# One operand of a seven-product matrix scheme gets a buffer of its own, two others are made at later tiles

## The chip, the cores and the metric

The kernel runs on one core of a Trainium2 chip. The metric is the device time of one execution in microseconds (us), here the median of several runs. "The trace" is one execution recorded by the hardware profiler; its times count from the first instruction.

## What is computed

For each of 8 batches of 512 tokens with 2048 features, a linear layer with a per-batch low-rank adapter is followed by a gated feed-forward block, and the input is added at the end:

```python
h   = x @ W.T + bias + (x @ A.T) @ B.T          # W: 2048x2048, A, B: rank 16, chosen by batch
q   = h @ Wq.T                                  # router: top 8 of 512 slots, softmax, values
aux = softmax(top8(...)) @ values @ Wvd.T @ Wvu.T
u   = 0.5 * log1p(var(h)) / mean(log1p(var)) + 2.5 * sigmoid(gelu(h @ Wu1.T + bu1) @ Wu2.T + bu2)
out = x + h + gate(u) * aux
```

All of it is in fp32. Only the first line matters for the change.

## The kernel before, in words

**The scheme.** W is cut into 2 x 2 blocks of 1024 x 1024. Two batches form a pair, so that x is a 2 x 2 block matrix too, and h is made with seven block products instead of eight, from sums and differences of blocks. There are four pairs. Each pair runs the products in the order M1, M2, M6, M7, M4, M5, M3 (lines 45 and 46), and each product has 8 output tiles of 128 rows. A tile g (0 to 223, `tile_of(g)` gives pair, product, tile) is 8 steps of k with three matmuls each (lines 1781 to 1783), since each fp32 operand is split into a high and a low part: high x high, high x low, low x high. The first tile of M1, M2, M7 and M4 also carries two matmuls of the adapter for each k (lines 1721 and 1722), and the tile after each tile of M2, M4, M5 and M3 carries one (line 1709).

**Differences of weight blocks.** M6, M7, M4 and M5 need differences of W's blocks, called T2, T3, T4 and T1. They are made once, in the first pair, in 8 pieces of 128 x 1024 (512 KB) each, and three of the four go to DRAM (`t_dram`) for the later pairs. `t_res` (32 KB a partition) holds W's first block for M1; `make_t1(o)` (line 1265) turns its piece o into T1, which ScalarE's queue stores (`store_t1`, line 895); `make_t2(o)` (line 1270) turns it into T2, which stays for M6. `make_t4(o)` (line 1275) computes T4 from a block of W and T2; `store_t4` (line 899) stores it; it is read again for M4. `make_t3(o)` (line 1280) makes T3 in the place of the tile's own weights, and `split_w_hi` stores it.

**The ring of raw weights.** All pieces of W, the loads for T1, T2 and T4 among them, go through `wraw`, a ring of three places of 512 KB. The list `entries` (lines 363 to 373) sets their order by due tile; load n goes to place n mod 3 and waits in SyncE's queue (`load_w`, line 531) until what lay there is used: for T1 and T2 until VectorE has made them, for T4 and T3 until their store to DRAM has landed (`wait_stored`, line 389). SyncE issues all loads in one order: at step g the `wraw` loads that are due by g + 1, a piece of `t_res` while g is under 6, the loads of x up to a given entry, and the adapter's. What waits first holds all behind it.

**A step of the engines.** Every engine runs its own list, tile by tile; its part for tile g is called step g here. ScalarE at step g writes the high part of the weights of tile g + 2 (`split_w_hi`, line 877; it waits until tile g - 1 is done, since `wsp` has three places), stores and squares the output of tile g - 2, stores T1 and T4 of step g - 1, and writes high parts of x for the next product (`PREP_AT`: k = 0, 1, 2, 3 at tiles 1, 2, 3, 5 of a product, k = 4 to 7 at its last tile). VectorE at step g adds up the outcome of tile g - 1 (`combine`), writes the low part of the weights of tile g + 2 (`split_w_lo`), makes the T pieces that are due, writes the low parts of x (`split_x_lo`), adds the sums of tile g - 2 to `sums` (`add_sums`, line 1349) and finishes tile g - 1 (`finish`, line 1328) where it is a tile of h. GpSimd makes the sums and differences of x. TensorE at tile g waits for the low part of its weights, in a first tile also for the low part of each x, and for a free bank.

**What is made when.** Lines 357 to 359 give the step at which VectorE makes each piece:

```python
T1_AT = dict(zip((1, 2, 3, 4, 5, 6, 9, 11), range(HT)))
T2_AT = dict(zip((8, 10, 12, 13, 14, 15, 16, 17), range(HT)))
T4_AT = {16 + o: o for o in range(HT)}
T3_AT = {M7 * HT - 3 + o: o for o in range(HT)}
```

In the first pair M1 is tiles 0 to 7, M2 8 to 15, M6 16 to 23, M7 24 to 31, M4 32 to 39. Tile 8 is the first that takes its weights from the ring; M6 (tiles 16 to 23) takes them from `t_res`.

**The sums.** `sums` holds two buffers of 4 KB a partition, one for each segment of h. M2 of the first pair is segment 1 and uses `sums[:, 1]`; `sums[:, 0]` is first written at VectorE's step 34, in M4.

Of the kernel before, what the change touches and what calls it, by code (L numbers as in the profile page):

```python
# [48 lines left out]
def bass_adaln_ffn(  # L49
# [35 lines left out]
    with ctx:  # L85
        def sem(name):
            return ctx.enter_context(nc.semaphore(name))
# [73 lines left out]
        t_res = at(at_t, "t_res", [P, HT, WT])  # L161
        stage = at(at_stage, "stage", [P, NST, 2, S])
        sums = at(at_sums, "sums", [P, 2, 2, S])
        a_sp = at(at_asp, "a_sp", [P, KT, 4, 2 * RANK], f32r)
        a_raw = at(at_lora, "a_raw", [P, 2, KT, RANK])
        b_raw = at(at_lora + 2 * K, "b_raw", [KL, S])
# [155 lines left out]
        ev_ready = sem("ev_ready")  # L322
        last6_ready = sem("last6_ready")
        pool6_ready = sem("pool6_ready")
        gated_act = sem("gated_act")
        last7_ready = sem("last7_ready")
        last_out = sem("last_out")
# [21 lines left out]
        def x_lo(i):  # L349
# [4 lines left out]

        T1_AT = dict(zip((1, 2, 3, 4, 5, 6, 9, 11), range(HT)))
        T2_AT = dict(zip((8, 10, 12, 13, 14, 15, 16, 17), range(HT)))
        T4_AT = {16 + o: o for o in range(HT)}
        T3_AT = {M7 * HT - 3 + o: o for o in range(HT)}  # L360


        entries = [(g, 1, "t1", o) for g, o in T1_AT.items()] + [(g, 1, "t2", o) for g, o in T2_AT.items()] \
            + [(g, 1, "t4", o) for g, o in T4_AT.items()]
        for g in range(TILES):
            p, q, o = tile_of(g)
            if q == M6 or (p == 0 and q == M1):
# [14 lines left out]

        def is_stored(n):
            kind, g = entries[n][2:4]
            return kind == "t4" or kind == "tile" and g < PAIR and tile_of(g)[1] == M7

        def wait_stored(eng, kind, g):
            n = W_PLACE[kind, g]  # L390
            eng.wait_ge(t_out[n % NWR], 16 * sum(is_stored(i) for i in range(n % NWR, n + 1, NWR)))

        def wait_all_stored(eng):
            for place in range(NWR):
                eng.wait_ge(t_out[place], 16 * sum(is_stored(i) for i in range(place, len(entries), NWR)))

        def t_count(what, o):
            order = [(g, 0, "t1", i) for g, i in T1_AT.items()] + [(g, 1, "t2", i) for g, i in T2_AT.items()] \
                + [(g, 2, "t4", i) for g, i in T4_AT.items()] + [(g, 3, "t3", i) for g, i in T3_AT.items()]
            return [e[2:4] for e in sorted(order)].index((what, o)) + 1  # L400


# [124 lines left out]
        def _(sp):  # L527
# [3 lines left out]
            def load_w(n):  # L531
                when, _, kind, g = entries[n]
                if n >= NWR:
                    _, _, old, og = entries[n - NWR]
                    if old == "tile":
                        p, q, o = tile_of(og)
                        sp.wait_ge(wl_ready, og + 1)
                        if p == 0 and q == M7:
                            wait_stored(sp, "tile", og)
                    elif old in ("t1", "t2"):  # L540
                        sp.wait_ge(t_ready, t_count(old, og))
                    elif old == "t4":
                        wait_stored(sp, "t4", og)
                    elif old == "wu":
                        sp.wait_ge(wul_ready, 2 * og + 2)
                    elif old == "wq":
                        sp.wait_ge(wql_ready, 1)
                into, done = wraw[:, n % NWR, :], w_in[n % NWR]
                if kind == "wu":
                    sp.dma_start(into.rearrange("p (k f) -> p k f", k=2),  # L550
                                 x[NB, 2 * g:2 * g + 2].rearrange("k p f -> p k f")).then_inc(done, 16)
                elif kind == "wq":
                    sp.dma_start(into.rearrange("p (k f) -> p k f", k=KT),
                                 w[0:KT, :, D:D + BOT].rearrange("k p f -> p k f")).then_inc(done, 16)
                elif kind == "wvu":
                    sp.dma_start(into, w[KT, :, g * WT:(g + 1) * WT]).then_inc(done, 16)
                elif kind == "t1":
                    sp.dma_start(into, w[HT + g, :, 0:WT]).then_inc(done, 16)
                elif kind == "t2":
                    sp.dma_start(into, w[HT + g, :, WT:2 * WT]).then_inc(done, 16)  # L560
                elif kind == "t4":
                    sp.dma_start(into, w[g, :, WT:2 * WT]).then_inc(done, 16)
                else:
                    p, q, o = tile_of(g)
                    if q == M2:
                        src = w[o, :, WT:2 * WT]
                    elif q == M1 or (p == 0 and q == M7):
                        src = w[o, :, 0:WT]
                    elif q == M3:
                        src = w[HT + o, :, WT:2 * WT]  # L570
                    else:
                        if q == M5:
                            sp.wait_ge(t_moved[o], 32)
                        elif p == 0:
                            wait_stored(sp, "t4", o)
                        else:
                            wait_all_stored(sp)
                        src = t_dram[{M7: T3, M4: T4, M5: T1}[q], o]
                    sp.dma_start(into, src).then_inc(done, 16)

            def load_x(n):
                name, p, k = x_entries[n]
# [98 lines left out]
            for g in range(TILES):  # L681
# [26 lines left out]
                while nx <= upto:  # L708
                    load_x(nx)
                    nx += 1  # L710
                ahead = g + 1
                if ahead < TILES:
                    ap, aq, ao = tile_of(ahead)
# [152 lines left out]
        def _(act):  # L866
# [31 lines left out]

            def store_t4(o):
                act.wait_ge(t_ready, t_count("t4", o))  # L900
                act.dma_start(t_dram[T4, o], w_raw("t4", o)).then_inc(t_out[W_PLACE["t4", o] % NWR], 16)

            def split_a_hi(p):
                act.wait_ge(a_in, 32 * (p + 1))
# [138 lines left out]
            for g in range(TILES):  # L1043
# [8 lines left out]
                    split_w_hi(g + 2)  # L1052
                if g > 1 and tile_of(g - 2)[1] in H_PRODUCTS:
                    square_and_store(g - 2)
                if g - 1 in T1_AT:
                    store_t1(T1_AT[g - 1])
                if g - 1 in T4_AT:
                    store_t4(T4_AT[g - 1])
                if (q, o) in B_SPLIT:
# [4 lines left out]
                if pp < NPAIR:  # L1064
                    for k in PREP_AT.get(o, ()):
                        split_x_hi(pp, pq, k)
                if g == LAST + M5 * HT:
                    values_copy()
                if g == LAST + M5 * HT + 1:
# [185 lines left out]
        def _(dve):  # L1255
# [17 lines left out]
                dve.tensor_tensor(t_res[:, o, :], w_raw("t2", o), t_res[:, o, :], SUB).then_inc(t_ready, 1)  # L1273

            def make_t4(o):
                wait_w(dve, "t4", o)
                dve.wait_ge(t_ready, t_count("t2", o))
                dve.tensor_tensor(w_raw("t4", o), w_raw("t4", o), t_res[:, o, :], SUB).then_inc(t_ready, 1)

            def make_t3(o):  # L1280
                g = M7 * HT + o
# [67 lines left out]
            def add_sums(g):  # L1349
# [4 lines left out]
                dve.wait_ge(sq_ready, n + 1)  # L1354
                if o == 0 and q in (M2, M4):
                    wait(dve, stats_done, seg - 1)
                    dve.tensor_copy(into, stage[:, n % NST, :, :]).then_inc(sum_ready, 1)
                else:
                    dve.wait_ge(sum_ready, n)
# [53 lines left out]
            for g in range(TILES):  # L1413
# [10 lines left out]
                    make_t1(T1_AT[g])  # L1424
                if g in T2_AT:
                    make_t2(T2_AT[g])
                if g in T4_AT:
                    make_t4(T4_AT[g])
                if g in T3_AT:
                    make_t3(T3_AT[g])  # L1430
                if (q, o) in B_SPLIT:
# [25 lines left out]
                    add_sums(g - 2)  # L1457
                if g > 0 and tile_of(g - 1)[1] in H_PRODUCTS:
                    finish(g - 1)
            add_sums(TILES - 2)  # L1460
            finish(TILES - 1)
            split_wu_lo(7)
# [573 lines left out]
```

## Time and profile before

| | |
|---|---|
| median of 3 runs | 1962.99 us (1960.79 to 1964.92) |
| the profiled execution, device time | 1958.85 us |
| its span, first to last instruction | 1957.1 us |
| TensorE busy | 1924.3 us (98%) |
| VectorE busy | 1250.9 us (64%) |
| ScalarE busy | 693.6 us (35%) |
| GpSimd busy | 407.1 us (21%) |
| mean granted clock of TensorE | 0.996 |
| DMA | 416.56 MB, mean 213 GB/s |

The shares are means over the whole span. In the page's 40 slices of 49 us, TensorE is busy 8 tenths in the first and 9 or more in the second, third and all others but the last; VectorE shows 8 tenths in the third slice; the DMA engines show 8 tenths in the first two. A share of TensorE near 100% says nothing on where its idle microseconds lie: for that the waits and the windows of single tiles are read. A tile's start is the start of the first of its 24 matmuls of lines 1781 to 1783 in TensorE's rows in order of time.

### The profile page before, as it was taken

Reading aid. Unit: us, or ns where it says so; the run is one execution under the profiler, and the core shown is the slowest. Engines: PE = TensorE matmul, PEld = TensorE weight load, DVE = VectorE, ACT = ScalarE, POOL = GpSimd, SP = SyncE. Lnnn points to the kernel's source line nnn. Section 1 sums busy time; section 2 is a strip of 40 time slices with the busy share of each in tenths; the row PEclk is TensorE's granted clock in tenths of the full one; section 3 lists DMA queues with packets and bytes.
Section 4 is the critical chain, followed back from the end, with each engine's and each line's share of the span. In section 5 each row is a group of like instructions: output and inputs, shape, how many; then the busy total and the mean of one; then the engine's idle time right before and its main releaser. Section 6 shows DMA issues by size and latency. Waiting matters only on the chain.

```text
span 1957.1 us, 24741 instructions
## 1 busy us (share of the span) xinstructions
PE 1924.3 (98%) x8618; PEld 1567.3 (80%) x8618; DVE 1250.9 (64%) x1639; ACT 693.6 (35%) x1059; POOL 407.1 (21%) x275
## 2 busy tenths in 40 slices
PE   8998999999999999999999999999999999999998
PEld 6776888888888888888888887778788888888886
DVE  5686587455468736546863644677566677676676
ACT  3332334333233433323333322345443233233332
POOL 2210132030023202002320200220343332332332
PEclk9998999999999999999999999999999999999999
DMA  8867677551367745146774424666888776777797
GB/s 289 287 241 243 219 243 231 160 178 58 133 207 234 230 150 170 65 148 211 231 226 143 164 90 169 227 219 213 284 270 273 249 237 226 242 236 234 239 359 285
DMA packets 196353, 416.56 MB, mean 213 GB/s; under 512 B 26820, under 2 KB 27844, under 8 KB 196102
## 3 DMA queue, kind: packets, MB, share of 16 engines
q1 hardware_dynamic: 150726, 325.83, 50.8%
q10 hardware_dynamic: 45504, 89.15, 12.0%
q8 instruction: 70, 1.15, 0.2%
q14 instruction: 53, 0.43, 0.1%
HBM read 317.37 MB, written 97.52 MB: 212 GB/s over the span
## 4 chain that ended last, share of the span: by engine, by line
PE 88%; issue 4%; DVE 3%; DMA 2%; ACT 1%; POOL 1%; SPq 1%; ACTq 0%; DVEq 0%; POOLq 0%
PE bank L1781 18%; PE bank L1782 18%; PE bank L1783 18%; PE bank L1817 6%; PE bank L1818 6%; PE bank L1819 6%; PE bank L1929 1%; PE bank L1931 1%; PE bank L1930 1%; PE bank L1709 1%; PE bank L1721 1%; PE bank L1722 1%; PE bank L1835 1%; PE bank L1834 1%; PE bank L1898 1%
## 5 line engine op out<-in xcount | busy, mean ns | idle before, releaser
L1781 PE MATMUL bank<-xop,wsp 128*128 128x512 f32 x1792 | 708.7, 395 | 19.7 <-DVE wsp L1257 10.7
L1782 PE MATMUL bank<-xop,wsp 128*128 128x512 f32 x1792 | 700.5, 391 | 0.0
L1783 PE MATMUL bank<-xop,wsp 128*128 128x512 f32 x1792 | 699.5, 390 | 0.0
L1781 PEld LDWEIGHTS bank<-xop,wsp 128*128 128x128 f32 x1792 | 337.5, 188 | 104.8 <-DVE xop L1257 11.1
L1782 PEld LDWEIGHTS bank<-xop,wsp 128*128 128x128 f32 x1792 | 337.7, 188 | 73.8 <-issue 3.8
L1783 PEld LDWEIGHTS bank<-xop,wsp 128*128 128x128 f32 x1792 | 337.3, 188 | 71.9
L868 ACT ACTIVATE wsp<-wraw 128x1024 fp32r<-128x1024 f32 x184 | 195.0, 1060 | 527.1 <-PE bank L1783 498.3
L1257 DVE TENSOR_TENSOR wsp<-wraw,wsp 128x1024 fp32r<-128x1024 f32 x184 | 232.2, 1262 | 192.7 <-ACT wsp L868 192.2
L850 POOL TENSOR_TENSOR r_h<-r_h,r_x 128x512 f32<-128x512 f32 x128 | 176.7, 1381 | 365.9 <-DMA r_h<-h_dram 325.2
L1817 PE MATMUL bank<-h_sp,wu 128*128 128x512 f32 x512 | 201.3, 393 | 2.1 <-DVE stage L1346 2.0
L1818 PE MATMUL bank<-h_sp,wu 128*128 128x512 f32 x512 | 200.4, 391 | 0.0
L1819 PE MATMUL bank<-h_sp,wu 128*128 128x512 f32 x512 | 199.8, 390 | 0.0
L1360 DVE TENSOR_TENSOR sums<-sums,stage 128x1024 f32<-128x1024 f32 x120 | 166.5, 1388 | 1.4 <-ACT stage L957 1.1
L813 POOL TENSOR_TENSOR xraw<-xraw 128x512 f32<-128x512 f32 x32 | 53.4, 1670 | 509.2 <-DMA xraw<-in_x 509.2
L1257 DVE TENSOR_TENSOR xop<-xraw,xop 128x512 fp32r<-128x512 f32 x184 | 151.1, 851 | 8.3 <-ACT xop L868 7.7
L1257 DVE TENSOR_TENSOR h_sp<-hraw,h_sp 128x512 fp32r<-128x512 f32 x128 | 106.6, 833 | 40.5 <-ACT h_sp L868 39.1
L1817 PEld LDWEIGHTS bank<-h_sp,wu 128*128 128x128 f32 x512 | 96.6, 189 | 23.6 <-DVE stage L1346 2.6
L1819 PEld LDWEIGHTS bank<-h_sp,wu 128*128 128x128 f32 x512 | 96.6, 189 | 20.9
L868 ACT ACTIVATE xop<-xraw 128x512 fp32r<-128x512 f32 x184 | 107.7, 617 | 13.9 <-POOL xraw L807 8.8
L1818 PEld LDWEIGHTS bank<-h_sp,wu 128*128 128x128 f32 x512 | 96.6, 189 | 19.7
L1605 DVE TENSOR_TENSOR o_st<-bank,r_h 128x512 f32<-128x512 f32 x96 | 66.0, 687 | 71.3 <-PE bank L1931 71.0
L807 POOL TENSOR_TENSOR xraw<-xraw,v_t 128x512 f32<-128x512 f32 x32 | 56.7, 1782 | 245.3 <-DMA xraw<-in_x 245.3
(172 smaller groups left out, 1950.7 us busy)
## 6 DMA issues: line engine op xcount, KB each, us to landing
xraw<-in_x SPq DMA_DIRECT2D x248, 256.0 KB, 4.1
wraw<-in_w SPq DMA_DIRECT2D x123, 512.0 KB, 3.8
wraw<-t_dram SPq DMA_DIRECT2D x88, 512.0 KB, 3.6
h_dram<-stage ACTq DMA_DIRECT2D x128, 256.0 KB, 2.7
hraw<-h_dram SPq DMA_DIRECT2D x128, 256.0 KB, 4.1
r_x<-in_x SPq DMA_DIRECT2D x128, 256.0 KB, 4.3
r_h<-h_dram SPq DMA_DIRECT2D x128, 256.0 KB, 3.5
out<-o_st ACTq DMA_DIRECT2D x96, 256.0 KB, 3.9
```

The lines of the kernel that those rows point to most:

```text
L807: pool.tensor_tensor(tile, tile, v_t[:, k, :], ADD).then_inc(s2_ready, 1)
L850: pool.tensor_tensor(r_h[:, n % 4, :], r_h[:, n % 4, :], r_x[:, n % 4, :], ADD).then_inc(r_ready, 1)
L868: return act.activation(dst, src, ACT.Copy)
L1257: return dve.tensor_tensor(dst, src, hi.bitcast(f32), SUB)
L1360: dve.tensor_tensor(into, into, stage[:, n % NST, :, :], ADD).then_inc(sum_ready, 1)
L1605: dve.tensor_tensor(o_st[:, a % 4, :], aux_bank[:], r_h[:, a % 4, :], ADD).then_inc(out_ready, 1)
L1781: pe.matmul(ps, wsp[:, slot, 0, f], x_hi(i), start=(k == 0), stop=False)
L1782: pe.matmul(ps, wsp[:, slot, 0, f], x_lo(i), start=False, stop=False)
L1783: last = pe.matmul(ps, wsp[:, slot, 1, f], x_hi(i), start=False, stop=(k == HT - 1))
L1817: pe.matmul(u_ps[m][:], wu[k][:, 0, f], h_sp[step % 4][:, 0, :], start=(k == 0), stop=False)
L1818: pe.matmul(u_ps[m][:], wu[k][:, 0, f], h_sp[step % 4][:, 1, :], start=False, stop=False)
L1819: last = pe.matmul(u_ps[m][:], wu[k][:, 1, f], h_sp[step % 4][:, 0, :], start=False, stop=(k == KT - 1))
```

## The change

T4 of the first pair leaves the ring: it gets `t4_raw`, the first half of `sums`, with two semaphores of its own, `t4_in` and `t4_out`. It is loaded by `load_t4` at the end of SyncE's step before the one in which it is made, after a wait for the store of the piece before. It is made every second step, at 14, 16, up to 28, at the very end of VectorE's step, after `finish`. T1 moves from steps 1 to 11 to steps 2 to 12, T2 from 8 to 17 to 13 to 20. The store of T1 moves to the end of ScalarE's step, behind the high parts of x; that of T4 stays at its place among ScalarE's instructions and now reads `t4_raw`. The first `add_sums` into `sums[:, 0]` waits for the last store of T4. The order in which `t_ready` is counted follows.

```diff
+        t4_raw = sums[:, 0, :, :].rearrange("p a s -> p (a s)")
...
-        T1_AT = dict(zip((1, 2, 3, 4, 5, 6, 9, 11), range(HT)))
-        T2_AT = dict(zip((8, 10, 12, 13, 14, 15, 16, 17), range(HT)))
-        T4_AT = {16 + o: o for o in range(HT)}
+        T1_AT = dict(zip((2, 4, 6, 8, 9, 10, 11, 12), range(HT)))
+        T2_AT = {13 + o: o for o in range(HT)}
+        T4_AT = {14 + 2 * o: o for o in range(HT)}
...
-        entries = [(g, 1, "t1", o) for g, o in T1_AT.items()] + [(g, 1, "t2", o) for g, o in T2_AT.items()] \
-            + [(g, 1, "t4", o) for g, o in T4_AT.items()]
+        entries = [(g, 1, "t1", o) for g, o in T1_AT.items()] + [(g, 1, "t2", o) for g, o in T2_AT.items()]
...
-            return kind == "t4" or kind == "tile" and g < PAIR and tile_of(g)[1] == M7
+            return kind == "tile" and g < PAIR and tile_of(g)[1] == M7
...
         def wait_all_stored(eng):
+            eng.wait_ge(t4_out, 16 * HT)
...
-                            wait_stored(sp, "t4", o)
+                            sp.wait_ge(t4_out, 16 * (o + 1))
...
+            def load_t4(o):
+                wait(sp, t4_out, 16 * o)
+                sp.dma_start(t4_raw, w[o, :, WT:2 * WT]).then_inc(t4_in, 16)
...
                 while nx <= upto:
                     load_x(nx)
                     nx += 1
+                if g + 1 in T4_AT:
+                    load_t4(T4_AT[g + 1])
...
             def store_t4(o):
                 act.wait_ge(t_ready, t_count("t4", o))
-                act.dma_start(t_dram[T4, o], w_raw("t4", o)).then_inc(t_out[W_PLACE["t4", o] % NWR], 16)
+                act.dma_start(t_dram[T4, o], t4_raw).then_inc(t4_out, 16)
...
-                if g - 1 in T1_AT:
-                    store_t1(T1_AT[g - 1])
                 if g - 1 in T4_AT:
                     store_t4(T4_AT[g - 1])
...
                     for k in PREP_AT.get(o, ()):
                         split_x_hi(pp, pq, k)
+                if g - 1 in T1_AT:
+                    store_t1(T1_AT[g - 1])
...
             def make_t4(o):
-                wait_w(dve, "t4", o)
+                dve.wait_ge(t4_in, 16 * (o + 1))
                 dve.wait_ge(t_ready, t_count("t2", o))
-                dve.tensor_tensor(w_raw("t4", o), w_raw("t4", o), t_res[:, o, :], SUB).then_inc(t_ready, 1)
+                dve.tensor_tensor(t4_raw, t4_raw, t_res[:, o, :], SUB).then_inc(t_ready, 1)
...
                     wait(dve, stats_done, seg - 1)
+                    if seg == 0:
+                        dve.wait_ge(t4_out, 16 * HT)
...
-                if g in T4_AT:
-                    make_t4(T4_AT[g])
...
                 if g > 0 and tile_of(g - 1)[1] in H_PRODUCTS:
                     finish(g - 1)
+                if g in T4_AT:
+                    make_t4(T4_AT[g])
```

## Rows read from the trace of the kernel before

**Rows 1.** TensorE's waits, whole span: us in total, times, longest.

```profile
PE bank L1781 <- DVE wsp L1257: 10.7, 3, 7.7
PE bank L1781 <- DVE xop L1257: 9.0, 3, 7.0
```

**Rows 2.** Single tiles as windows: stretch, us, busy by engine, granted clock, DMA share, GB/s.

```profile
47.95:54.57 6.62, 5.61 (x26) 4.35 (x24) 1.37 (x2) 2.47 (x4) 0.00 (x0) 1.00 0.64 257
60.13:70.98 10.85, 9.58 (x41) 6.49 (x40) 5.39 (x6) 4.80 (x7) 3.34 (x2) 1.00 0.83 309
110.86:117.62 6.76, 5.99 (x26) 4.62 (x25) 6.76 (x8) 3.78 (x6) 2.04 (x1) 1.00 0.85 290
128.50:136.06 7.56, 5.60 (x25) 4.34 (x24) 5.97 (x7) 1.58 (x2) 0.00 (x0) 1.00 0.47 190
147.06:152.50 5.44, 5.44 (x25) 4.50 (x24) 4.62 (x5) 1.06 (x1) 0.00 (x0) 1.00 0.67 231
157.94:176.92 18.98, 12.00 (x42) 8.23 (x40) 11.87 (x14) 4.46 (x7) 0.00 (x0) 0.73 0.63 223
215.02:224.19 9.17, 9.17 (x42) 6.65 (x40) 2.42 (x3) 1.06 (x1) 3.02 (x2) 1.00 0.56 184
229.91:235.60 5.69, 5.69 (x26) 4.70 (x25) 4.34 (x5) 2.62 (x4) 1.28 (x1) 1.00 0.87 303
```

**Rows 3.** TensorE in order of time at the longest wait: start, us, instruction, idle before.

```profile
169.66 0.80 PE L1781 MATMUL bank<-xop,wsp 128*128 128x512 f32 x1 [6.98 <-DVE xop L1257]
```

**Rows 4.** The chain that ended last, 45 to 180 us: start, us, what.

```profile
160.22 2.66 DMA t_dram<-wraw
162.94 3.69 DMA wraw<-in_w
```

**Rows 5.** SyncE's queue, its own waits, 100 to 176 us: total, times, longest.

```profile
SPq L560 <- DMA t_dram<-wraw: 13.5, 1, 13.5
SPq L579 <- DMA t_dram<-wraw: 12.5, 4, 5.4
```

**Rows 6.** SyncE's and ScalarE's rows in order of time, 28 to 61 us.

```profile
28.74 0.33 SPq L558 DMA_DIRECT2D wraw<-in_w  x1
...
46.21 0.43 SPq L617 DMA_DIRECT2D t_res<-in_w  x1
...
52.10 1.06 ACT L868 ACTIVATE wsp<-t_res 128x1024 fp32r<-128x1024 f32 x1 [8.79 <-DMA t_res<-in_w]
...
60.06 0.80 SPq L602 DMA_DIRECT2D xraw<-in_x  x2
```

**Rows 7.** VectorE in order of time, 94 to 121 us.

```profile
94.71 2.32 DVE L1273 TENSOR_TENSOR t_res<-wraw,t_res 128x1024 f32<-128x1024 f32 x1
...
109.76 0.74 DVE L1346 SCALAR_TENSOR_TENSOR stage<-bank,bias_sb,u_t 128x512 f32<-128x512 f32 x1
...
112.69 3.58 DVE L1257 TENSOR_TENSOR xop<-xraw,xop 128x512 fp32r<-128x512 f32 x4
...
120.25 1.21 DVE L1278 TENSOR_TENSOR wraw<-wraw,t_res 128x1024 f32<-128x1024 f32 x1
```

**Rows 8.** DMA issues, median us to landing, stretches 60:75, 75:95 and 115:160 in turn.

```profile
t_dram<-t_res ACTq DMA_DIRECT2D x1, 512.0 KB, 7.3
...
wraw<-in_w SPq DMA_DIRECT2D x7, 512.0 KB, 5.7
t_dram<-t_res ACTq DMA_DIRECT2D x2, 512.0 KB, 5.4
...
wraw<-in_w SPq DMA_DIRECT2D x9, 512.0 KB, 3.8
t_dram<-wraw ACTq DMA_DIRECT2D x7, 512.0 KB, 3.7
```

**Rows 9.** The stretches of M2 and of M6 as windows, columns as in Rows 2.

```profile
60.13:110.86 50.73, 49.46 (x216) 39.38 (x215) 39.76 (x37) 19.07 (x26) 15.02 (x9) 1.00 0.87 311
110.86:157.94 47.08, 44.35 (x194) 36.07 (x193) 34.77 (x38) 13.40 (x18) 2.04 (x1) 1.00 0.66 226
```

More of the change, by code:

```diff
@@ L324, in bass_adaln_ffn @@
         pool6_ready = sem("pool6_ready")
+        t4_in = sem("t4_in")
+        t4_out = sem("t4_out")
         gated_act = sem("gated_act")
@@ L398, in t_count @@
             order = [(g, 0, "t1", i) for g, i in T1_AT.items()] + [(g, 1, "t2", i) for g, i in T2_AT.items()] \
-                + [(g, 2, "t4", i) for g, i in T4_AT.items()] + [(g, 3, "t3", i) for g, i in T3_AT.items()]
+                + [(g, 2, "t3", i) for g, i in T3_AT.items()] + [(g, 3, "t4", i) for g, i in T4_AT.items()]
             return [e[2:4] for e in sorted(order)].index((what, o)) + 1
@@ L541, in load_w @@
                         sp.wait_ge(t_ready, t_count(old, og))
-                    elif old == "t4":
-                        wait_stored(sp, "t4", og)
                     elif old == "wu":
@@ L560, in load_w @@
                     sp.dma_start(into, w[HT + g, :, WT:2 * WT]).then_inc(done, 16)
-                elif kind == "t4":
-                    sp.dma_start(into, w[g, :, WT:2 * WT]).then_inc(done, 16)
                 else:
```

## The prediction

> **What bounds the kernel now.** I read TensorE's waits over the whole span first. Two groups on the weights and on x name VectorE's low parts: 10.7 us and 9.0 us, three waits each [rows 1]. The 7.7 us in the first is the start of the kernel. All the others lie in the first pair; from the second pair on TensorE has no wait of these kinds. So the change, which touches little but the first pair, can give back what the first pair loses and no more.
>
> Next I took the lengths of tiles as windows [rows 2], since a tile's length also holds the pick-up after a wait and a lowered clock. An undisturbed tile takes 5.44 us, one with one adapter matmul 5.69, a first tile with sixteen 9.17. Against these, five tiles are long: tile 6 by 1.18 (6.62 - 5.44), tile 8 by 1.68 (10.85 - 9.17), tile 16 by 1.07 (6.76 - 5.69), tile 19 by 2.12 (7.56 - 5.44) and tile 24 by 9.81 (18.98 - 9.17). Together that is 15.86 us, 0.8% of the span: **the ceiling of the gain**. Tile 24 holds 6.98 us of waiting for x's low part [rows 3]; the rest, 2.8 us, is mostly the clock: the granted clock over this tile is 0.73, where the other seven windows show 1.00 [rows 2].
>
> Then the causes. For tile 24 the chain [rows 4] alternates between a store to `t_dram` (2.66), a load into `wraw` (3.69) and VectorE, three times over: T4 and T3 pass through three places, each freed only when its store has landed, and SyncE issues in order. Its queue waited 13.5 us in one wait at line 560 (a load for T2 behind a store of T4, which is the wait of tile 19) and 12.5 us in four at line 579 (the weights of M7) [rows 5]. For tiles 6 and 8 the cause is the early loads of T1: the first load for T1 that reuses a place goes at 28.74, after VectorE made the first T1; behind it come `t_res` 5 to 7. `t_res` 7 is issued at 46.21, ScalarE waits 8.79 us for it, and the last x for M2 goes at 60.06 [rows 6], tile 8 running since 60.13. For tile 16, VectorE's low parts of x start at 112.69 and take 3.58 for four, while tile 16 wants the first of them 4 x 0.68 us after 110.86, at 113.6. VectorE is late there by about 6 us: it finishes tile 13 from 109.76 to 110.5 [rows 7], the end of its step 14, and this needs only the adapter's matmul behind k = 5 of tile 14, which started at 99.5 (110.86 - 2 x 5.69), so that it could end at 104.5.
>
> **The change, part by part.** All times are against the profiled execution (span 1957.1, device 1958.85, which lies 4.1 us below the median of the runs, 1962.99).
>
> *T1 late.* No work is added or removed. SyncE's steps 0 to 5 issue three T1 loads instead of six (of the eight in all), and up to step 4 neither waits for a place. So `t_res` 5 to 7 are no longer behind T1's making, and VectorE's steps 1 and 3, whose low part of x frees the next x place, lose a T1 of 1.2 to 2.3 us. By my estimate `t_res` 7 then goes 4 to 7 us earlier (two or three T1 pieces of 1.2 to 2.3 each ahead of it on VectorE), against a delay of 1.2 to be recovered; x for M2 follows. Gain 1.18 + 1.68 = **2.9 us**; bounds 1.5 (only tile 6, and a little) to 2.9. What is late next there: nothing in the rows is within 4 us.
>
> *M2 pays for it.* Five T1 stores instead of three now fall in M2, with ten loads for T1, T2 and T4 instead of nine, and one store of T4. I count 21 pieces of 0.524 MB (5 of weights, 8 of T1 and T2, 2 loads and 1 store of T4, 5 stores of T1) and 22 of 0.262 MB (x, `s2`, h): 16.8 MB in 8 tiles of 48.9 us, 343 GB/s. Before it was 311 GB/s at a DMA share of 0.87 [rows 9], which scales to 357 at a full share: M2 comes to 96% of that. So landings there get no shorter than 5.7 us for a load [rows 8]. The stores of T1 stand behind x in ScalarE's list, so they hold nothing. A T1 or T2 load must land within a step (5.69) of VectorE's freeing its place, so VectorE will run behind as before. But it starts M2 on time, where before its step 8 began only after tile 8's late x; I take 3 to 4 us instead of 6. At tile 16, T4's first piece adds one instruction at the end of step 14: 1.21 us, or 2.3 where GpSimd works beside it [rows 7]; 3.5 + 1.2 to 2.3 stays just under the old lag of 6. The 1.07 us of tile 16 therefore goes mostly: **gain 0.5**, bounds +1.07 and -2.5 (old lag kept, T4 at 2.3, another 1.3 from the full DMA).
>
> On the durations 1.21 and 2.32 for the same shape, the Trainium skill (GPSIMD Engine Reference, Key points) says that GpSimd shares its SBUF interfaces with VectorE and contends with it on instructions with two SBUF inputs. By it T4 in M2 would cost the longer value, in M6 and M7 the shorter, as GpSimd is busy for 2.04 us in all of M6 [rows 9]; the sum would be 1.1 us worse at most.
>
> *T2 late.* T2 piece o is made one step before `split_w_hi(16 + o)` wants it (two to seven steps before). ScalarE now waits for it: with VectorE 4 us behind, high part 16 comes some 2 us later than before. Queued behind it are the store and square of h, the T4 store and x's high parts. TensorE wants the weights of tile g + 2 at 10.88 us after tile g starts, and they are ready at 1.06 + 1.23 = 2.3, so 8.6 us cover it. Cost 0; if VectorE fell 9 us behind it would show in full.
>
> *T4 in its own place.* Removed: eight loads and eight waits for stores in the ring. T3's own cycle over three places stays: store 3.7 and load 3.8 [rows 8] against three steps of 5.44. Added: a round trip for each T4, store, load, make: 3.7 + 3.8 + 1.22 = 8.7 us, with two issues about 9.5, against two steps, 10.88. Waiting for `t4_in` stands last in VectorE's even steps; behind it are the next step's combine, weights' low part, T2 or T3 and x. In SyncE's queue `load_t4` waits for the store before; behind it stands the next T2 or T3 load. With the lag that M2 leaves, I estimate that T4's second piece has landed in DRAM 10 us after tile 17 starts; T2 piece 6 is loaded behind it and lands 4 us into tile 19, where it is wanted at 3. VectorE is then 4 to 5 us late at each even step's end, within the 8.6. At tile 24, x's part 4 should be ready about 1.3 us after its start and is wanted at 4 x 1.14 = 4.6; no T4 falls in step 23. So the waits of tiles 19 and 24, with the lowered clock, go: **gain 2.12 + 9.81 = 11.9**; bounds 6 (a wait of 3 us left at tile 24, with its clock) and 11.9. Late next would be x's part 4 of tile 24, by a margin of 3 us.
>
> On T4 the Trainium skill speaks against the change: its page Trainium Kernel Development and Optimization (Best Practices) asks to double-buffer so that DMA and compute overlap, and one place for T4 makes store, load and make follow one another. By that rule the round trip would show. Its page DMA: Bandwidth & Descriptors (Anatomy of one DMA) gives about 2.0 us plus bytes over 436 GB/s, 3.2 us for 512 KB: as an estimate 1.2 + 2 x 3.2 = 7.6 us a round, still under two steps.
>
> *The rest.* The wait for `t4_out` at step 34 comes five steps after the last store: 0. Places of the ring shift for the later pairs: 0, as loads keep their order.
>
> Sum: 2.9 + 0.5 + 11.9 = 15.3; I take 0.3 off for pick-ups left over: **15.0 us**. Span 1942.1, profiled time 1943.9, and on the scale of the runs 1963.0 - 15.0 = **1948.0 us**. Own range: 1945 (all of 15.9 and 2 of scatter) to 1952.
>
> **Rivals.** (1) *A wait takes the place of the one removed*: SyncE's blocking moves from T4's places to `load_t4`, so that weights of M7 still come late. For it: five T4 loads stand between M7's loads and each waits for a store. Against it: 9.5 against 10.88. A wait of 3 us at tile 24 with 2.8 of clock leaves 9: 1963 - 9 = 1954 us.
>
> (2) *M2 becomes bound by DMA*: at 96% of what it can move, landings pass 6.8 us (two landings and 3.5 us of work in three steps of 5.69), and waits of 3 to 4 us come at tiles 12 to 16. For it: share 0.87 already; against it: the store work is spread over five steps. 15.3 - 4 = 11.3: 1951.7 us.
>
> (3) *Slower: T4's round trip over its single place.* If it takes longer than two steps, each of the seven further pieces adds the excess, to VectorE and through `load_t4` to SyncE. At the longest values seen, 7.3 for a store, 5.7 for a load and 2.3 for the make [rows 7, 8], it is 15.3 us, 4.4 too long: 7 x 4.4 = 31, less 8.6 of cover, plus 2.8 of clock = 25; less the 15.9 saved = +9.6: 1972.6 us. It decides from a round trip of 10.88 + (15.9 - 2.8 + 8.6)/7 = 14.0 us.
>
> (4) *It doesn't do what it says*: the late loads come from full DMA engines, not from the places, and the time stays: 1963 +- 3. Against it: in M6 the share is 0.66 [rows 9] while SyncE waits 13.5 us on one store [rows 5].
>
> **How the numbers follow.** Forecast 0.62, rival 1 0.13, rival 2 0.12, rival 4 0.05, rival 3 0.08. The range runs from 1944 to 1956 and holds the first three, 0.87 less some scatter. 0.2% is 3.9 us, about what runs of this kernel can tell from no change. Faster by more: 0.87, less 0.02 for a mix of rivals, 0.85. Within: 0.07. Slower: 0.08.
>
> **What would show it.** Right: tile lengths near 5.44, 5.69 and 9.17 in all of tiles 6 to 24, no clock under 1.00 at tile 24, SyncE's waits at lines 560 and 579 on stores gone but for T3's, T4 made every second tile with its round trip under 10.9 us, `t_res` 7 issued near 40 us. Wrong for M2: waits at tiles 12 to 16 and a DMA share near 1. Wrong for T4: VectorE idle for `t4_raw` for more than 3 us at each even step. The prediction would be wrong if a wait long enough to lower the clock remained at a first tile.

## The result and the profile after

The changed kernel takes 1944.08 us in the median (1942.44 to 1944.71), the kernel before beside it 1962.88 (1960.79 to 1964.92). The ratio is 0.9906, 95% interval 0.9891 to 0.9921: 18.8 us faster, with 15.0 forecast. The traced execution has a span of 1942.6 us against 1957.1, which is 14.5 less; the prediction had the span at 1942.1.

These are the tiles that were long before, as windows of the trace after (stretch, us, busy of TensorE, its weight loads, VectorE, ScalarE and GpSimd, granted clock, DMA share, GB/s): tiles 6, 8, 16, 19, the undisturbed tile 22, and tile 24. They answer to [rows 2].

```profile
48.50:53.94 5.44, 5.44 (x26) 4.51 (x24) 4.28 (x5) 1.84 (x3) 0.00 (x0) 1.00 0.51 174
59.38:68.55 9.17, 9.17 (x42) 6.65 (x40) 4.08 (x3) 1.74 (x3) 2.59 (x2) 1.00 0.65 233
108.42:114.44 6.02, 5.98 (x26) 4.62 (x25) 6.02 (x8) 2.87 (x5) 1.18 (x1) 1.00 1.01 353
125.32:130.76 5.44, 5.44 (x25) 4.51 (x24) 5.44 (x6) 1.69 (x2) 0.00 (x0) 1.00 0.67 270
141.64:147.08 5.44, 5.44 (x25) 4.51 (x24) 4.19 (x4) 1.06 (x1) 0.00 (x0) 1.00 0.73 266
152.52:161.69 9.17, 9.17 (x41) 6.66 (x40) 5.06 (x7) 1.31 (x2) 0.00 (x0) 1.00 0.74 216
```

Four of the five are at the length of an undisturbed tile of their kind; tile 16 keeps 6.02 - 5.69 = 0.33 us. Tile 24 is 9.17 instead of 18.98, at clock 1.00 instead of 0.73. The sum over the five is 1.18 + 1.68 + 0.74 + 2.12 + 9.81 = 15.5. M4 (tile 32) starts at 199.80 instead of 215.02, 15.2 us earlier: the first tile is 0.4 us longer and starts 0.1 later, and tiles 7 and 20 lose 0.12 us less each. From there to the end it is 1742.8 us against 1742.1.

SyncE's own waits between 100 and 176 us (total, times, longest) answer to [rows 5]. Line 583 is the load of T4, line 394 the wait for T3's store:

```profile
SPq L583 <- DMA t_dram<-sums: 48.7, 6, 11.4
SPq L394 <- DMA t_dram<-wraw: 17.9, 3, 6.4
```

SyncE now waits longer on T4's stores than before, 48.7 us, but no longer in front of the weights when these are due.

VectorE around tile 16 and at T4's last two pieces (start, us, instruction, idle before) answers to [rows 7]:

```profile
105.01 0.74 DVE L1352 SCALAR_TENSOR_TENSOR stage<-bank,bias_sb,u_t 128x512 f32<-128x512 f32 x1
...
171.33 1.22 DVE L1284 TENSOR_TENSOR sums<-sums,t_res 128x1024 f32<-128x1024 f32 x1
...
184.40 1.22 DVE L1284 TENSOR_TENSOR sums<-sums,t_res 128x1024 f32<-128x1024 f32 x1 [2.71 <-DMA sums<-in_w]
```

Tile 13 is finished at 105.7. Tile 14 started at 97.04, and 5.0 us later (the 104.5 less 99.5 of the prediction) would be on time: VectorE is 3.7 us behind, where it was 6. And T4's last round, make to make, took 13.1 us; VectorE stood idle for its load for 2.71 of them.

The DMA issues (median us to landing) from 75 to 95 and from 95 to 115 us, against [rows 8]:

```profile
wraw<-in_w SPq DMA_DIRECT2D x8, 512.0 KB, 7.1
t_dram<-t_res ACTq DMA_DIRECT2D x4, 512.0 KB, 7.6
...
wraw<-in_w SPq DMA_DIRECT2D x4, 512.0 KB, 8.2
t_dram<-t_res ACTq DMA_DIRECT2D x1, 512.0 KB, 9.1
```

Landings in M2 did grow, from 5.7 to 7 or 8 us for a load. And the windows of M2, M6 and M7 (columns as above), against [rows 9]:

```profile
59.38:108.42 49.04, 49.04 (x216) 39.56 (x215) 36.44 (x35) 17.59 (x25) 15.04 (x9) 1.00 0.85 312
108.42:152.52 44.10, 44.06 (x194) 36.17 (x193) 41.07 (x46) 16.16 (x22) 1.18 (x1) 1.00 0.71 260
152.52:199.80 47.28, 47.28 (x210) 38.20 (x208) 30.97 (x35) 13.56 (x17) 1.67 (x1) 1.00 0.87 295
```

TensorE is busy for all of M2 and M7 and all but 0.04 us of M6. The ends of matmuls are modelled in the trace, so tile 16's 0.33 us show in its length and not as idle time.

### The profile page after: what moved, and what is told of

Read it like the earlier page. It is cut to its first block, busy times and chain, and to the rows that moved or that the text cites. A ratio compares the mean times of both kernels' runs of the same rounds, so it can differ in the third digit from the quotient of the medians.

```text
span 1942.6 us, 24742 instructions
## 1 busy us (share of the span) xinstructions
PE 1920.2 (99%) x8618; PEld 1566.4 (81%) x8618; DVE 1251.7 (64%) x1639; ACT 694.0 (36%) x1059; POOL 394.7 (20%) x275
## 4 chain that ended last, share of the span: by engine, by line
PE 95%; DVE 2%; ACT 1%; DMA 1%; issue 1%; SPq 0%; ACTq 0%; DVEq 0%
PE bank L1789 20%; PE bank L1790 20%; PE bank L1791 20%; PE bank L1825 6%; PE bank L1826 6%; PE bank L1827 6%; PE bank L1729 2%; PE bank L1730 2%; PE bank L1937 1%; PE bank L1939 1%; PE bank L1938 1%; PE bank L1717 1%; PE bank L1843 1%; PE bank L1842 1%; PE bank L1906 1%; PE bank L1898 1%
## 5 line engine op out<-in xcount | busy, mean ns | idle before, releaser
L1827 PE MATMUL bank<-h_sp,wu 128*128 128x512 f32 x512 | 199.8, 390 | 0.0
L1263 DVE TENSOR_TENSOR xop<-xraw,xop 128x512 fp32r<-128x512 f32 x184 | 162.2, 911 | 4.8 <-ACT xop L874 4.3
L1368 DVE TENSOR_TENSOR sums<-sums,stage 128x1024 f32<-128x1024 f32 x120 | 164.3, 1369 | 1.4 <-ACT stage L963 1.1
L1263 DVE TENSOR_TENSOR h_sp<-hraw,h_sp 128x512 fp32r<-128x512 f32 x128 | 101.2, 791 | 40.4 <-ACT h_sp L874 38.8
```

What stands on the lines that cost most here:

```text
L1263: return dve.tensor_tensor(dst, src, hi.bitcast(f32), SUB)
L1368: dve.tensor_tensor(into, into, stage[:, n % NST, :, :], ADD).then_inc(sum_ready, 1)
L1827: last = pe.matmul(u_ps[m][:], wu[k][:, 1, f], h_sp[step % 4][:, 0, :], start=False, stop=(k == KT - 1))
```

## The experiments

In the tables of single tiles, "excess" is a tile's length less 5.44, 5.69 or 9.17 us, by its kind, as in the prediction. Every kernel was run several times beside the kernel before and traced; a reading of single tiles below rests on one trace, unless it is said otherwise.

**The kernel before, once more.** No edit.

> The kernel before, unchanged, once more, to see what its waits do from one execution to the next. The runs moved by 18.8 us in the median, while the one traced execution of either kernel moved by 14.5 us in span. Theory A (waits of the first pair scatter): the five long tiles of the first pair lose more than 15.9 us in an execution near the median, most of it at tile 24 by a wait on a DMA that lands later, 18 to 20 us together. Theory B (the difference lies elsewhere): the five tiles lose 15 to 17 us again and the rest of the span is the longer one. Ratio to the kernel before 1.000 in both.

Median 1961.69 (1955.44 to 1963.29), ratio 0.9998 (0.9983 to 1.0013). Its tiles 6, 8, 16, 19 and 24:

```profile
49.05:55.02 5.97, 5.61 (x25) 4.35 (x24) 1.37 (x2) 2.47 (x4) 0.00 (x0) 1.00 0.64 258
60.58:73.40 12.82, 9.71 (x41) 6.49 (x40) 7.31 (x7) 4.79 (x7) 2.94 (x2) 1.00 0.73 264
113.28:120.46 7.18, 6.05 (x26) 4.62 (x25) 7.18 (x8) 3.78 (x6) 1.96 (x1) 1.00 0.86 299
131.37:138.76 7.39, 5.60 (x25) 4.34 (x24) 5.97 (x7) 1.58 (x2) 0.00 (x0) 1.00 0.46 188
160.61:179.53 18.92, 10.73 (x41) 7.43 (x40) 12.08 (x14) 4.45 (x7) 0.00 (x0) 0.82 0.61 213
```

Excess 0.53, 3.65, 1.49, 1.95 and 9.75: 17.4 us against 15.9 in the first trace. M4 starts at 217.63, 2.6 us later. But the span is 1955.5, as the rest is shorter, 1737.9 against 1742.1. The five tiles' 17.4 us lie between theory A's 18 to 20 and theory B's 15 to 17, and this execution (1957.49) is no more a typical one than the first. Theory A is right in direction only (the waits of the first pair scatter by microseconds, at tile 8 above all, not at tile 24), and the rest of the span scatters by as much, which neither theory had. Of the 2.6 us at M4's start, 1.1 are a later end of the first tile.

**T4's place alone.** T1 and T2 at their old steps, T1's store at its old place.

```diff
-        T1_AT = dict(zip((2, 4, 6, 8, 9, 10, 11, 12), range(HT)))
-        T2_AT = {13 + o: o for o in range(HT)}
+        T1_AT = dict(zip((1, 2, 3, 4, 5, 6, 9, 11), range(HT)))
+        T2_AT = dict(zip((8, 10, 12, 13, 14, 15, 16, 17), range(HT)))
```

> Only T4's place of its own, with T4 made at steps 14, 16 to 28; T1 and T2 are made and stored where the kernel before has them. Theory A (T4 in the ring makes the waits of tiles 19 and 24): these go, 11.9 us, tiles 6 and 8 keep theirs of 2.9, tile 16 grows by 1 to 2 since T4's first piece stands at the end of step 14: about 1952 us, 10 to 12 below before. Theory B (the gain needs T2's and T1's new steps, since they too crowd the ring in tiles 8 to 17): tile 24 keeps a wait, and less than 6 us are gained.

Median 1946.74 (1944.27 to 1948.69), ratio 0.9923 (0.9902 to 0.9945): 15.6 us below the kernel before beside it, where theory A had 10 to 12. Most of the gain is T4's place. Its tiles 8 and 16, the only two with an excess from tile 1 to tile 32:

```profile
59.26:69.94 10.68, 9.53 (x42) 6.50 (x41) 5.41 (x6) 4.80 (x7) 3.40 (x2) 1.00 0.86 316
109.81:117.68 7.87, 5.99 (x26) 4.62 (x25) 7.87 (x10) 4.11 (x6) 0.76 (x1) 1.00 0.72 247
```

Tiles 19 and 24 have none, tile 8 keeps 1.51, tile 16 grows from 1.07 to 2.18, as theory A had it. M4 starts at 203.03, 12.0 us earlier than in the first trace of before and 14.6 earlier than in the second. Tile 6 has no excess here although T1 is at its old steps.

**T1 late alone, T4 in the ring.**

```diff
-        T1_AT = dict(zip((1, 2, 3, 4, 5, 6, 9, 11), range(HT)))
+        T1_AT = dict(zip((2, 4, 6, 8, 9, 10, 11, 12), range(HT)))
```

> Only T1 at steps 2, 4, 6, 8 to 12; T2, T4 and the ring as before. Theory A: tiles 6 and 8 lose their 2.9 us, tile 16 may lose its 1.1, tiles 19 and 24 keep 11.9: 1959 to 1960 us. Theory B (starting M2 on time also gets T4 and T2 through the ring earlier): tile 24's wait shrinks with the 2.9 us by which VectorE is earlier, 1955 us or less.

Median 1961.5 (1957.22 to 1968.15), ratio 0.9998 (0.9986 to 1.0011): nothing gained. Both theories were wrong. Tiles 14, 15, 16 and 24:

```profile
96.33:103.46 7.13, 5.85 (x26) 4.54 (x25) 6.38 (x5) 1.93 (x3) 1.69 (x1) 1.00 0.63 210
103.46:109.89 6.43, 5.98 (x26) 4.62 (x26) 5.96 (x6) 2.12 (x4) 2.68 (x2) 1.00 0.98 320
109.89:122.86 12.97, 8.68 (x25) 6.62 (x26) 12.74 (x12) 4.87 (x8) 4.25 (x3) 0.74 0.87 326
162.03:180.31 18.28, 11.07 (x41) 7.62 (x40) 12.07 (x14) 4.45 (x7) 0.00 (x0) 0.81 0.61 212
```

Tiles 6 and 8 have lost their excess, but 1.4, 0.7 and 7.3 us appear at tiles 14 to 16, the last with a lowered clock. Steps 8 to 12 now hold T1 pieces and some of T2 as well, each a load, a place in the ring and an instruction in the same tile. The chain from 90 to 125 us (start, us, what) goes through them, and at its end through a load of x:

```profile
89.29 7.63 DMA wraw<-in_w
...
98.08 2.32 DVE t_res L1273
100.42 3.49 DMA wraw<-in_w
...
112.41 4.71 DMA xraw<-in_x
```

Line 1273 makes T2. So the pieces of T1 and T2 are in the path of tile 16's wait; whether their number in a step or the full DMA engines (share 0.98 in tile 15) makes the loads late was not taken apart. The 2.9 us at tiles 6 and 8 can't be had by moving T1 into T2's steps.

**T1 and T2 late, T4 in the ring.** T1's store stays at its old place in ScalarE's step.

```diff
-        T1_AT = dict(zip((1, 2, 3, 4, 5, 6, 9, 11), range(HT)))
-        T2_AT = dict(zip((8, 10, 12, 13, 14, 15, 16, 17), range(HT)))
+        T1_AT = dict(zip((2, 4, 6, 8, 9, 10, 11, 12), range(HT)))
+        T2_AT = {13 + o: o for o in range(HT)}
```

> T1 and T2 at their new steps, but T4 in the ring of three places at steps 16 to 23 as before. Theory A: T2 pieces are now queued behind T4 stores from step 16 on, and ScalarE wants each one step later: tile 24 keeps its wait of 7 us and tiles 19 to 23 get waits of 2 us and more: 1960 to 1972 us. Theory B (the late steps are what brings the gain): 1950 us or less.

Median 1970.87 (1968.36 to 1975.6), ratio 1.005 (1.0034 to 1.0065): slower by 9 us. Tiles 16, 23 and 24:

```profile
108.38:117.72 9.34, 7.54 (x27) 5.78 (x25) 9.34 (x12) 4.40 (x7) 1.99 (x1) 0.82 0.77 268
158.82:168.16 9.34, 5.71 (x25) 4.43 (x25) 4.79 (x5) 1.06 (x1) 0.00 (x0) 0.99 0.58 194
168.16:190.73 22.57, 12.98 (x40) 8.88 (x41) 12.07 (x14) 4.44 (x7) 0.00 (x0) 0.70 0.66 228
```

Excess 3.65 at tile 16, 12.4 over tiles 19 to 23 (3.9 of it in tile 23), 13.4 at tile 24. SyncE's queue waited at the loads for T2 on stores of T4:

```profile
SPq L560 <- DMA t_dram<-wraw: 36.7, 4, 13.5
```

So the new steps by themselves are harmful, and the place is worth 228.8 - 199.8 = 29 us with them (28 against the kernel below that has T1's store at its old place too), 12 to 15 without. The change is one whose parts can't be added up.

**T4 at every step.** Changed kernel, with the pace doubled.

```diff
-        T4_AT = {14 + 2 * o: o for o in range(HT)}
+        T4_AT = {14 + o: o for o in range(HT)}
```

> The changed kernel with T4 made at every step from 14 to 21 instead of every second; everything else as changed. Theory A (one place costs a round trip of 8 to 9.5 us for each piece: store 2.7 to 4, load 3.7 to 5, make 1.2): it no longer fits into one tile of 5.44, each of the seven further pieces is 2.6 to 4 us late, about 23 in all; VectorE's cover takes up 5 to 9, so tiles 17 to 24 lose 13 to 18 us: 1957 to 1962 us. Theory B (the round trip is hidden behind other work in any case, as VectorE and ScalarE go on): under 3 us lost, 1944 to 1947 us.

Median 1960.93 (1958.41 to 1964.14), ratio 1.0003 (0.9991 to 1.0014): the whole gain is gone, as theory A had it. The chain that ended last (start, us, what) names the round trip piece by piece:

```profile
110.06 5.34 DMA xraw<-in_x
...
119.92 1.23 DVE sums L1284
121.17 2.65 DMA t_dram<-sums
123.83 3.71 DMA sums<-in_w
127.56 1.23 DVE sums L1284
128.82 2.65 DMA t_dram<-sums
131.48 3.62 DMA sums<-in_w
```

One round is 7.6 us: 1.2 to make, 2.65 to store, 3.7 to load. In this stretch the tiles take that time, not their own:

```profile
138.23:145.95 7.72, 5.72 (x25) 4.43 (x25) 4.70 (x6) 1.69 (x2) 0.00 (x0) 1.00 0.58 204
145.95:153.60 7.65, 7.32 (x24) 5.55 (x25) 4.69 (x6) 1.06 (x1) 0.00 (x0) 0.78 0.59 205
```

Tiles 17 to 23 lose 13.7 us, close to six rounds of 7.65 - 5.44 = 2.2. Tile 24 loses 2.9 and tile 16 6.5: the chain goes there through a load of x issued at 110.06, which in SyncE's order stands behind the second T4 load and its wait.

**T4 from step 16.** Changed kernel, all of T4 two steps later.

```diff
-        T4_AT = {14 + 2 * o: o for o in range(HT)}
+        T4_AT = {16 + 2 * o: o for o in range(HT)}
```

> The changed kernel with T4 made at steps 16, 18 to 30 instead of 14 to 28, so that M2 holds none before its last tile. Theory A (the last wait of the first pair, 0.33 us at tile 16, and the risk there come from T4's first piece at the end of step 14): the wait goes, 0.3 us less, which the runs can't tell: 1943.8, the trace can. Theory B (it comes from the full DMA engines in M2): a wait of 0.3 us or more stays at tile 16.

Median 1941.06 (1938.6 to 1942.36), ratio 0.9903 (0.9887 to 0.992). Tile 16:

```profile
107.55:113.24 5.69, 5.69 (x26) 4.70 (x25) 5.69 (x8) 3.12 (x6) 0.00 (x0) 1.00 0.91 322
```

Its wait is gone, and with it the last excess of the first pair, with the DMA share still at 0.91: theory A.

**T1 stored twice.** Changed kernel, with a second copy of each T1 piece, for more DMA work in M2.

```diff
+    spare = nc.dram_tensor("spare", (HT, P, WT), f32, kind="Internal").ap()
...
                 act.dma_start(t_dram[T1, o], t_res[:, o, :]).then_inc(t_moved[o], 16)
+                act.dma_start(spare[o], t_res[:, o, :]).then_inc(t_moved[o], 16)
...
-                dve.wait_ge(t_moved[o], 32)
+                dve.wait_ge(t_moved[o], 48)
```

> The changed kernel with every piece of T1 stored to DRAM a second time, to a place nobody reads; T2 waits for both. That puts 2.6 MB more through the DMA engines in M2, 19.4 MB in 49 us or 396 GB/s. Theory A (the engines move at most some 350 to 360 GB/s here, and M2 of the changed kernel is just within it): the excess is 5 to 7 us, VectorE's lag of 3.6 us grows past its cover, and tiles 12 to 16 wait 2 to 6 us: 1946 to 1950 us. Theory B (landings grow but nothing is short): no wait but tile 16's, 1944 to 1945 us.

Median 1943.97 (1943.2 to 1944.6), ratio 0.9917 (0.99 to 0.9933). Tile 16 and all of M2 as windows, then what the DMA engines moved from 95 to 115 us, and the issues there:

```profile
108.77:116.96 8.19, 6.49 (x26) 4.46 (x25) 7.96 (x8) 3.40 (x6) 3.56 (x2) 1.00 1.00 375
59.87:108.77 48.90, 48.90 (x216) 39.39 (x215) 33.40 (x33) 17.18 (x23) 12.17 (x7) 1.00 0.93 349
```

```profile
DMA packets 3096, 8.25 MB, mean 413 GB/s; under 512 B 351, under 2 KB 351, under 8 KB 3096
...
wraw<-in_w SPq DMA_DIRECT2D x2, 512.0 KB, 11.3
...
t_dram<-t_res ACTq DMA_DIRECT2D x1, 512.0 KB, 13.4
```

For 20 us the engines moved 413 GB/s, with landings of 11 to 13 us for the ring's loads and T1's stores, and TensorE did not wait in M2. Tile 16 lost 2.5 us, 2.2 more than in the changed kernel. The wait lies in theory A's range, at one tile only; the time, 1943.97, is at the low end of theory B's. A's reason is refuted: the engines do not stop at 350 to 360 GB/s. The traces of before and of the changed kernel show that too, in stretches of 9 and 10 us of M2:

```profile
97.50:106.50 9.00, 9.00 (x41) 7.43 (x40) 8.78 (x9) 3.31 (x5) 3.24 (x2) 1.00 1.02 398
...
95.00:105.00 10.00, 10.00 (x46) 8.25 (x44) 8.49 (x7) 2.96 (x4) 3.54 (x3) 1.00 1.04 413
```

**T4's place and T2 late, T1 as before.** Changed kernel with T1's steps and the place of T1's store of before.

```diff
-        T1_AT = dict(zip((2, 4, 6, 8, 9, 10, 11, 12), range(HT)))
+        T1_AT = dict(zip((1, 2, 3, 4, 5, 6, 9, 11), range(HT)))
```

> T4's place and T2's new steps, T1 at its old steps and its store at the old place. Together with the run of T4's place alone and the changed kernel it splits the 3 us between T2 and T1. Theory A (T1's new steps take tile 8's wait of 1.5, T2's take tile 16's of 2.2): tile 8 keeps 1.5 to 2, tile 16 has under 0.5: 1945 to 1946 us. Theory B (all of it is T1's, through the time at which M2 starts): both waits stay, 1946.7 us.

Median 1943.13 (1941.75 to 1944.68), ratio 0.991 (0.9894 to 0.9927). Tile 8 keeps an excess of 0.49, tile 6 one of 0.20, tile 16 has none; M4 starts at 200.39. The time is 2 us under theory A's range. Theory A for T2: in the traces its late steps, beside T4's place, take away tile 16's 2.2 us; the two ratios, with intervals of 0.9902 to 0.9945 and 0.9894 to 0.9927, don't tell the kernels apart. For T1 the theory has the right tile and too large a value: its new steps take away 0.7 us here, and 199.80 or 200.61 (next run) against 200.39 is no difference.

**The changed kernel and T4 from step 16, again, on one chip.** No edit, and the edit of above.

> The changed kernel, unchanged, beside the variant with T4 from step 16 on the same chip, since the kernel before has had medians of 1960.5 to 1962.9 us in the three comparisons so far. Theory A (the first pair without long waits scatters little, and what is left of scatter lies where the products end and the feed-forward steps begin): ratio 0.990 to 0.992, first pair ending within 1 us of 199.8, tile 16 with a wait under 1 us. Theory B (tile 16's wait varies like the long ones did): it takes 2 us or more in some execution, and the first pair ends over 201.

> The variant with T4 at steps 16, 18 to 30 once more, on the same chip as the changed kernel. Theory A (T4's first piece in M2 costs 0.3 us): 0.3 us below the changed kernel, not told apart by the runs. Theory B (the 3 us between the medians of the two in different comparisons are real): 2 to 3 us below it.

Changed: 1942.65 (1941.71 to 1946.86), ratio 0.9912 (0.9898 to 0.9927), M4 at 200.61, tile 16 with 0.36. T4 from 16: 1943.48 (1942.09 to 1945.34), ratio 0.9912 (0.9897 to 0.9927), M4 at 200.52, tile 16 with none. Theory A in both: the 3 us between 1944.08 and 1941.06 came from different comparisons, in which the kernel before had 1962.88 and 1960.51. The variant takes 0.36 us of waiting off a trace and can't be told from the changed kernel by time.

**The order in ScalarE's step.** T4's store behind the high parts of x (the diff: at the end of the step, after T1's), and, in the other kernel, T1's store ahead of them, at T4's side.

```diff
-                if g - 1 in T4_AT:
-                    store_t4(T4_AT[g - 1])
...
                 if g - 1 in T1_AT:
                     store_t1(T1_AT[g - 1])
+                if g - 1 in T4_AT:
+                    store_t4(T4_AT[g - 1])
```

> The changed kernel with T4's store behind ScalarE's high parts of x, where the change in words puts it and its code doesn't. Theory A (the round trip of T4, 7.7 us where nothing else holds it, has 3.2 us of room in two tiles): the store goes out 0.7 us later in most odd steps and 2.4 later at tile 23, all within the room: same as the changed kernel, 0.990 to 0.992. Theory B (the store is on the path through VectorE's wait for T4): 2 us or more are lost in tiles 24 to 31.

> The changed kernel with T1's store ahead of the high parts of x again, as in the kernel before. Theory A (a store is an issue of 0.4 us on ScalarE, which has room in M2, as VectorE is the one that runs behind): no difference, 0.990 to 0.992. Theory B (ScalarE must wait there for T1 to be made before it can write x's high part, and VectorE waits for that part): tiles 12 to 16 get a wait of 1 us or more.

T4's store last: 1944.89 (1942.67 to 1947.4), ratio 0.9921 (0.9905 to 0.9938). T1's store early: 1943.43 (1941.84 to 1944.96), ratio 0.9912 (0.9897 to 0.9927). Tile 16 of the one and of the other:

```profile
108.34:115.13 6.79, 6.00 (x27) 4.62 (x25) 6.79 (x8) 2.37 (x4) 0.80 (x1) 1.00 0.76 268
...
108.09:115.24 7.15, 6.00 (x26) 4.62 (x25) 7.15 (x9) 3.48 (x5) 2.28 (x1) 1.00 0.89 318
```

Excess 1.10 and 1.46 against 0.33 and 0.36, nothing elsewhere; in tiles 24 to 31 there is none in either. For T4's store theory A holds but for tile 16, which it did not name; for T1's store both are half right, one wait over 1 us at tile 16 and no difference in time. By the runs both kernels are the same as the changed one; the order may be worth 1 us at tile 16, on one trace each.

## Why the prediction was right, and where it was off

**The ceiling and its reading** held for the trace: the losses sat in five tiles of the first pair, and these gave 15.5 of the 15.9 us. The slices of the page point there as well, which the section on the profile before has wrong: TensorE and its clock show 8 tenths in the fourth slice, 147 to 196 us, where tile 24 waits. What failed is taking one execution's losses for the kernel's. The second trace of before loses 17.4 in the same tiles. Even that leaves part of the 18.8 us between the medians open: the two traced executions of before, 1957.1 and 1955.5 in span, lie 4 to 5 us below its medians of 1962.9 and 1961.7 with the 1.8 us around a span counted, so what its typical execution loses was not traced. That it is more waiting in the first pair is likely, and not shown. The runs give one hint: of the 22 executions of before in the first comparison of the experiments, the four with the lowest mean granted clock, 0.994, take 1963.9 us on average and the four with the highest, 0.997, 1959.2, while the traced ones have 0.996 and 0.998. So the longer executions tend to spend more time at the lowered clock; where, no trace shows. For this reason the measured time, 1944.08, is under the prediction's own range (1945 to 1952) and only 0.1 us inside its wider one (1944 to 1956). That it is inside by 0.1 us is luck: the mechanism was right, and the size of the gain was read from an execution that was faster than most.

**T1 late, 2.9 us.** The size came out in the pair of traces (1.18 + 1.68). In all ten traces with T1's new steps tiles 6 and 8 have no excess, and `t_res` 7 was issued at 41.28, inside the 4 to 7 us forecast. But as a cause it was over-sized: without T1's new steps, T4's place and T2's steps left only 0.7 there, and the waits scatter from 0.5 to 3.7 at tile 8 between traces with T1 at its old steps. Alone, the step gains nothing, because it collides with T2's steps; the prediction did not say that the two moves need each other. T1's new steps beside T4's place, with T2 as before, were not run. By time, T4's place alone (ratio 0.9902 to 0.9945) can't be told from the whole change (0.9891 to 0.9921, and 0.9898 to 0.9927 again): what the new steps of T1 and T2 add to it is seen in single traces only.

**M2 pays.** VectorE's lag was given as 3 to 4 us and is 3.7; tile 16 gained 0.74 where 0.5 was forecast. T4's piece in M2 took 1.65 us, between the 1.21 and the 2.3 weighed for it, with GpSimd busy beside it up to 106.2; those in M6 and M7 took 1.21 to 1.23. Both sides of the sum on the DMA engines are mis-sized. M2 was to move 343 GB/s and moved 312: 19 pieces of 512 KB and 20 of 256 KB were issued in it, not 21 and 22. And the limit of 357 GB/s, from scaling a share of 0.87 to 1, is no limit: the run with T1 stored twice moved 413 GB/s, the trace of before 398 for 9 us, and landings past 6.8 us, which rival 2 called the point of waits at tiles 12 to 16, came (7.1 to 8.2) without more than the 0.33 us of tile 16. The likely reason that they cost nothing, argued and not tested, is that M2's few tiles are over before the lag has used up the 8.6 us of cover. Rival 2 is refuted for the changed kernel; with 2.6 MB more tile 16 loses 2.2 us more, on one trace.

**T2 late, cost 0.** Right beside T4's place, where M4 even starts 2.6 us earlier (203.03 to 200.39, one trace each). In the ring it costs: M4 starts 10.4 us later than with T1 late alone (218.42 to 228.84). In the kernel before T2's pieces are made four to six steps ahead of their use, not two to seven as the prediction has it; its sum does not use this.

**T4 in its own place, 11.9 us.** Right in size, place and cause: the run with the place alone gained 12.0 us at M4's start against the first trace, with tiles 19 and 24 clean. The round trip was forecast at 9.5 and is 7.6 with nothing in its way. In M7 the last round was longer than forecast, 13.1, over two steps of 10.88 and over the prediction's own sign of being right: its store and its load took 5.6 us each to land, with the DMA share of M7 at 0.87. No tile of M7 is longer for it; that VectorE's cover of 8.6 us hid it is argued. Rival 1 did not come: SyncE waits 48.7 us on T4's stores and the weights of M7 are still in time. Rival 3's mechanism is real and was shown by making T4 at every step: each round then costs its excess over the pace, and in addition SyncE's order passes the wait on to x. Its condition does not hold in M6, and in M7 for too few rounds. (Its price was added up 0.3 us too high: 31 - 8.6 + 2.8 - 15.9 is 9.3, not 9.6.) Of the two rules of the Trainium skill weighed there, double-buffering (Trainium Kernel Development and Optimization, Best Practices) did not decide at this pace; it did at twice the pace. The estimate from the Trainium skill's page DMA: Bandwidth & Descriptors (Anatomy of one DMA), 7.6 us a round, agrees with the 7.6 measured in the sum; by part it has 3.2 and 3.2 where the trace has 2.65 for the store and 3.7 for the load. That section of the Trainium skill gives its fit for DMAs issued from GpSimd, and T4's are issued by SyncE and ScalarE, so the agreement of the sum may be chance.

**The stores' order.** Only T1's store was moved behind the high parts of x; the run with both moved shows no gain that is missed by it.

## What to carry to other kernels

A buffer that is filled, changed, stored and filled again needs no second copy if its uses stand further apart than its round trip (here they are 10.9 us apart, with a round trip of 7.6 and only at the end of 13.1); what hurts is when such a buffer shares a ring with loads that have deadlines, because its slow release then sets theirs. Measure the round trip once (make, store, load) and space the uses by it, and check what stands behind its wait in the loader's queue. Moving work to later steps was useless or harmful while the ring was shared, and did no harm once it wasn't, so test such parts alone and together, and take the ceiling of a gain from more than one trace.

## What the runs showed of the hardware that was not expected

The DMA engines moved 413 GB/s for 20 us, while the windows of M2 at a share of 0.85 to 0.87 moved 311 or 312. Windows of a few microseconds with a share of 1.00 to 1.04 moved 353, 375, 398 and 413 GB/s: a share near 1 does not name one rate, and a smaller one can't be scaled to a limit. Landings of 512 KB went from 3.7 us to 11 to 13 us there.

Executions of one kernel differ by 4 to 5 us after the first pair, 1737.9 to 1742.1 us from tile 32 to the end for the kernel before, and 1742.8 and 1744.3 for the changed one. Part of it sits where the products end and the feed-forward steps begin. TensorE's wait for the first low parts of h there, in the second trace of before and in the second of after (total, times, longest), and a window of 30 us around it in each, with the wait ending 19 us after its start:

```profile
PE bank L1842 <- DVE h_sp L1257: 2.9, 1, 2.9
...
PE bank L1850 <- DVE h_sp L1263: 5.2, 1, 5.2
```

```profile
1364.00:1394.00 30.00, 25.45 (x111) 20.40 (x110) 20.52 (x24) 10.93 (x19) 6.46 (x5) 1.00 0.62 206
...
1350.00:1380.00 30.00, 22.76 (x86) 17.56 (x85) 17.18 (x22) 10.97 (x19) 6.34 (x5) 0.89 0.61 210
```

After the wait of 5.2 us the granted clock of the stretch is 0.89 (0.50 from 1369 to 1374 us), with that of 2.9 it is 1.00: a wait there can cost more than itself, as at tile 24. The length of a wait alone doesn't decide it. In the first trace of before two waits end there, of 1.99 us at 1373.3 and of 2.46 at 1382.0; the clock is 0.83 from 1370 to 1380 and 1.00 from 1380 to 1390. The difference in the rest is not an effect of the change: T4 from step 16 showed 1738.1 us for the rest in one trace and 1743.0 in the next. Why the wait's length scatters was not tried.
